# A post-norm transformer layer on 8 cores: the first layernorm's scaling moved out of the row block and into the FFN's accumulation

## What is computed

```python
# layer input x: [16, 2048, 1024]
a = window_attention(x)      # 16 heads of 64, 2 kv heads, window of 256 rows,
                             # softmax without scaling, then @ Wo + bo
x = layernorm(x + a)         # (v - mean) / sqrt(var + 1e-5), no gain, no offset
# FFN: complex linear map, 512 real + 512 imaginary features, no nonlinearity
W_real = unfold(G1_R, G2_R); W_imag = unfold(G1_I, G2_I)        # 512 x 512 each
out_real = x_real @ W_real.T - x_imag @ W_imag.T + bias_real
out_imag = x_real @ W_imag.T + x_imag @ W_real.T + bias_imag
x = layernorm(x + concat(out_real, out_imag))
```

## Time and profile before

| | us |
|---|---|
| median of 3 runs | 1385.72 (1383.74 to 1406.99) |
| the profiled execution | 1384.69, its span on the slowest core (core 2) 1383.1 |
| spans of the eight cores | 1373.1 to 1383.1 |
| mean granted TensorE clock, all cores | 0.75 |
| prologue, until the first scores | 229.7 |

### The profile page before, as it was taken

One profiled execution on the slowest core, in us unless ns is written; L12 is line 12 of the kernel. 1 busy time (PEld: TensorE's weight loads), 2 busy tenths in 40 slices (PEclk: granted clock), 3 DMA queues, 4 the chain that ended last, 5 costly groups with the idle time before them and its releaser, 6 DMA issues.

```text
span 1383.1 us, 17008 instructions; the slowest of 8 cores (1373.1 to 1383.1 us)
## 1 busy us (share of the span) xinstructions
PE 810.7 (59%) x4568; PEld 358.3 (26%) x4568; DVE 557.3 (40%) x1539; ACT 396.1 (29%) x673; POOL 359.3 (26%) x324
## 2 busy tenths in 40 slices
PE   0077333766577666676756476757486557665653
PEld 0033000322233223232222232323232223222321
DVE  0001444355505551455554111455415541555553
ACT  3333113322323322333320234323233223322310
POOL 0000002434304340343430103343214430343410
PEclk9998555677777777877777686777687767777776
DMA  5520000000100001000000300000200020000000
GB/s 135 175 67 31 0 0 1 1 16 31 56 21 17 16 31 61 16 17 16 21 27 16 107 31 1 2 30 17 77 1 17 31 71 7 16 17 31 16 16 31
DMA packets 15869, 44.51 MB, mean 32 GB/s; under 512 B 3091, under 2 KB 5539, under 8 KB 15782
## 3 DMA queue, kind: packets, MB, share of 16 engines
q0 software_dynamic: 9216, 33.56, 6.9%
q1 hardware_dynamic: 6566, 9.87, 2.6%
HBM read 26.65 MB, written 16.78 MB: 31 GB/s over the span
## 4 chain that ended last, share of the span: by engine, by line
PE 52%; DVE 21%; issue 10%; DMA 8%; ACT 5%; POOL 2%; DVEq 1%; SPq 0%; ACTq 0%; POOLq 0%
PE pW L637 11%; PE pW L764 10%; PE pW L411 9%; PE pS L562 5%; DVE scr L650 5%; DMA xs<-x 5%; DVE attn L590 4%; PE pS L505 4%; PE pT L612 2%; PE pT L735 2%; DVE pre L783 2%; DVE x_tm L715 2%; PE pW L768 2%; DVE pre L680 1%; PE pW L641 1%
## 5 line engine op out<-in xcount | busy, mean ns | idle before, releaser
L523 ACT ACTIVATE EX<-pS,expbias 128x512 bf16<-128x512 f32 x384 | 242.6, 682 | 334.0 <-PE pS L505 333.5
L539 POOL TENSOR_TENSOR EX<-EX,maskl_s 128x512 bf16<-128x512 bf16 x128 | 150.7, 1199 | 417.2 <-ACT EX L523 417.2
L539 POOL TENSOR_TENSOR EX<-EX,maskr_s 128x512 bf16<-128x512 bf16 x128 | 172.3, 1369 | 275.0 <-ACT EX L523 274.4
L637 PE MATMUL pW<-wo_sb,attnT 128*128 128x512 bf16 x512 | 174.0, 502 | 34.6 <-DVE pre L783 33.3
L411 PE MATMUL pW<-XT,wq_sb 128*128 128x512 bf16 x512 | 130.6, 423 | 9.0 <-DVE XT L391 9.0
L735 PE MATMUL pT<-identb,x_tm 128*128 128x128 bf16 x256 | 31.2, 298 | 170.7 <-DVE x_tm L715 170.7
L650 DVE SCALAR_TENSOR_TENSOR scr<-pre 128x1024 bf16<-128x1024 f32 x64 | 122.0, 1906 | 6.7
L381 PE MATMUL pT<-identb,x_tm 128*128 128x128 bf16 x256 | 32.0, 304 | 156.0 <-ACT x_tm L371 142.8
L590 DVE TENSOR_SCALAR attn<-pS,Rrec 128x64 bf16<-128x64 f32 x512 | 110.2, 278 | 14.3 <-DVE attn L590 0.5
L505 PE MATMUL pS<-QT,KT 64*128 64x512 bf16 x384 | 102.5, 472 | 13.1 <-ACT EX L523 11.5
L580 DVE RECIPROCAL Rrec<-pS 128x4 f32<-128x4 f32 x128 | 23.3, 182 | 183.6 <-PE pS L562 183.2
(11 more groups left out here) (81 smaller groups left out, 764.3 us busy)
## 6 DMA issues: line engine op xcount, KB each, us to landing
xs<-x POOLq DMA_DIRECT2D x32, 512.0 KB, 4.6
y<-outst POOLq DMA_DIRECT2D x32, 512.0 KB, 3.0
wstage<-wq SPq DMA_DIRECT2D x4, 512.0 KB, 4.0
xs<-wq SPq DMA_DIRECT2D x4, 512.0 KB, 4.5
wstage<-wo SPq DMA_DIRECT2D x4, 512.0 KB, 4.4
xs<-wo SPq DMA_DIRECT2D x4, 512.0 KB, 4.5
wstage<-wk SPq DMA_DIRECT2D x1, 512.0 KB, 4.4
xs<-wv SPq DMA_DIRECT2D x1, 512.0 KB, 4.6
```

Of the source, the lines that this page charges most:

```text
L523: i = sca.activation(EX[:, exi * 512:(exi + 1) * 512], pS[quad % 2][:, :], AF.Exp, bias=expbias[:])
L539: i = gps.tensor_mul(EX[:, exi * 512:(exi + 1) * 512], EX[:, exi * 512:(exi + 1) * 512], m[:]) \
L637: ten.matmul(pW[half][:, :], attnT[:, ring * 1024 + c * 128: ring * 1024 + (c + 1) * 128], wo_sb[:, c * 1024 + half * 512: c * 1024 + (hal ...
```

## The change

The row block is no longer normalised before the FFN. With p the sum x + attention output (kept in bf16 as pre1b), m its mean and r its rstd, the FFN of the normalised rows is r * (p W - m (column sums of W) + beta / r), and a layernorm behind it doesn't see the factor r but in its epsilon. So:

- `x1norm_unit` and x1_tm are gone; the transposes read pre1b, and wait for the add alone. pre1b is bf16 where pre1 was fp32.
- `rstd1_unit` gets three small VectorE operations: -m and 1/r are written side by side as bf16 (spair).
- A new `statT_unit`, ahead of FFN half 0, transposes the two columns on TensorE into one row in pT, and VectorE copies the 256 values to srow.
- Each FFN half gets one more matmul with one contraction row (-m times the column sums of the weights, wbar_row), and the bias is multiplied by 1/r in place of 1.
- The second layernorm's statistics get three small VectorE operations more (the variance times r squared, plus epsilon) and one after rstd2 (r2c = rstd2 * rstd1).
- At the end of `emit_wbuild`, once: 16 matmuls with a column of ones and two ScalarE copies make wbar_row; the first waits for wrt, wit and witn.

```diff
+            for half in range(2):
+                if cur == "t":
+                    E.wait(E.res("pW0b")["f"])
+                    E.wait([ev_wrt, ev_wit, ev_init_v])
+                for c in range(8):
+                    ...
+                    i = ten.matmul(pW[0][0:1, :], ones_col[:],
+                                   wsrc[:, wc * 512:(wc + 1) * 512],
+                                   start=(c == 0), stop=(c == 7)) if cur == "t" else None
+                ev_mm = E.inc("t", i if cur == "t" else None)
+                if cur == "s":
+                    E.wait(ev_mm)
+                    i = sca.copy(wbar_row[0:1, half * 512:(half + 1) * 512], pW[0][0:1, :])
...
         def ln1_unit(b, S):
...
+                    if half == 0:
+                        E.wait(rx1["f"])
                 i = vec.scalar_tensor_tensor(
-                    pre1[:, ring * 1024 + half * 512: ring * 1024 + (half + 1) * 512],
+                    pre1b[:, ring * 1024 + half * 512: ring * 1024 + (half + 1) * 512],
...
+            rx1["r"] = ev_add
...
         def rstd1_unit(b, S):
...
+                vec.tensor_copy(spair[:, ring * 2: ring * 2 + 1], st1[:, c0 + 3:c0 + 4])
+                i = vec.reciprocal(st1[:, c0 + 4:c0 + 5], rstd1[:, ring:ring + 1])
...
+                i = vec.tensor_copy(spair[:, ring * 2 + 1: ring * 2 + 2],
+                                    st1[:, c0 + 4:c0 + 5])
-        def x1norm_unit(b, S):
...
+        def statT_unit(b, S):
+            ring = S % 2
+            rpt = E.res("pT")
+            i = None
+            if cur == "t":
+                E.wait(E.ev[f"spair_{ring}"])
+                E.wait(rpt["f"])
+                ten.transpose(pT[0:1, 0:128], spair[:, ring * 2: ring * 2 + 1],
+                              identb[:])
+                i = ten.transpose(pT[0:1, 128:256], spair[:, ring * 2 + 1: ring * 2 + 2],
+                                  identb[:])
+            ev_tr = E.inc("t", i if cur == "t" else None)
+            i = None
+            if cur == "v":
+                E.wait(ev_tr)
+                i = vec.tensor_copy(srow[0:1, ring * 256: ring * 256 + 256],
+                                    pT[0:1, 0:256])
+            ev_ev = E.inc("v", i)
+            rpt["f"] = ev_ev
+            E.ev[f"srow_{ring}"] = ev_ev
...
         def x1t_unit(b, S):
...
-                                  x1_tm[:, ring * 1024 + c * 128: ring * 1024 + (c + 1) * 128],
+                                  pre1b[:, ring * 1024 + c * 128: ring * 1024 + (c + 1) * 128],
...
         def ffn_unit(b, S, half):
...
+                E.wait(E.ev[f"srow_{ring}"])
...
-            i = ten.matmul(pW[half][:, :], ones_row[:],
+            ten.matmul(pW[half][:, :], srow[0:1, ring * 256: ring * 256 + 128],
+                       wbar_row[0:1, half * 512:(half + 1) * 512],
+                       start=False, stop=False) if cur == "t" else None
+            i = ten.matmul(pW[half][:, :], srow[0:1, ring * 256 + 128: ring * 256 + 256],
                            beta_row[0:1, half * 512:(half + 1) * 512],
                            start=False, stop=True) if cur == "t" else None
...
         def ln2out_unit(b, S):
...
+            extras = [
+                lambda: vec.tensor_tensor(st2[:, c0 + 4:c0 + 5], rstd1[:, ring:ring + 1],
+                                          rstd1[:, ring:ring + 1], ALU.mult),
+                lambda: vec.tensor_tensor(st2[:, c0 + 5:c0 + 6], st2[:, c0 + 6:c0 + 7],
+                                          st2[:, c0 + 4:c0 + 5], ALU.mult),
+                lambda: vec.tensor_scalar(st2[:, c0 + 6:c0 + 7], st2[:, c0 + 5:c0 + 6],
+                                          1.0, EPS, ALU.mult, ALU.add),
+            ]
...
+                i = vec.tensor_tensor(r2c[:, ring:ring + 1], rstd2[:, ring:ring + 1],
+                                      rstd1[:, ring:ring + 1], ALU.mult)
...
                 if 0 <= Q2 < 16:
+                    statT_unit(b, Q2)
                     ffn_unit(b, Q2, 0)
...
                     rstd1_unit(b, P)
-                    x1norm_unit(b, P)
```

83 lines of the change are left out of this document (47 added, 36 removed).

## The result

The changed kernel takes 1473.97 us (median of 10 runs) where the kernel before takes 1385.21 beside it: ratio 1.0643, 95% interval 1.0627 to 1.066. In some executions the cores of one die show a lower granted clock and take a few per cent longer; ratios leave these out. The sign of the forecast holds, its size doesn't: 1430 with a range to 1450. The profiled execution has spans of 1463.3 to 1474.7 us and a mean granted clock of 0.72 where it was 0.75.

A forecast was written before the change was run, and what follows sets the result against it. Waits between engines, then TensorE's clock, were taken to bound the kernel. Covered steps 24, steps after QKV 5.7, batch ends 1 and prologue 14 gave 45 us on 1384.69: 1430 us, +3.2%; range 1396 to 1450 at about 0.85.

The forecast's parts named there:

- the exponentials start at 439.8, as before: One loop step: the square waits only for the first mask and ends at 438.1 (before 438.03), so exponentials are not delayed.
- the 0.4 us that were to be gained before the FFN: One loop step: with normalisation and its wait gone, the FFN starts at 443.5 instead of 443.93.
- the clock's term: Covered steps: the hole ahead of the FFN delays the fast clock by 1.6 to 2.4 us, costing 0.95 us each.
- rival A: The clock rises as before despite the 0.75 us hole ahead of the FFN: 1407 us, +1.5%; chance 0.28.
- If the rise counts from the FFN's start: Clock in one step: counted from the FFN's start at 443.5, the rise comes at 447.0 to 447.8 instead of 445.4.
- Transposes of the statistics to FFN: Ahead of FFN half 0: the two new statistics transposes and their copy cost 0.96 us (0.69 to 1.3).
- The one-row matmuls: One added 512-column matmul in each FFN half: 0.23 us fast each, 0.46 us for a step.
- The prologue: Column sums of the weights ahead of the first scores, paid once: 14.0 us, or 10.6 at the fast clock.
- Steps with a QKV block: Steps after a QKV block, 4 of 32: hole 0.96 plus matmuls 0.46, 1.4 us each, 5.7 in all.
- Batch ends: Four steps at the ends of the two batches: +0.7 for the last, -0.3 for the one before, about 1 us in all.
- B: Rival: the clock doesn't fall at all in TensorE's wait, saving 2.2 us in 24 steps: 1354 us, -2.3%; chance 0.05.
- C: Rival: first layernorm's square runs at twice the rate on 16-bit inputs, 0.53 us less: 1394 or 1417; with A 0.08.

The follow-up runs named there:

- c_delay: Kernel before plus only the change's delay: three one-column VectorE operations behind the second layernorm's variance, one behind its rstd; 1400.5 us, ratio 1.0125.
- b_stat: Kernel before plus only the statistics pair, its two transposes, the copy and the FFN's wait for it, the row unused; 1412.7 us, ratio 1.0217.
- b_k1: Kernel before with each FFN half's bias matmul done twice, one more one-row matmul of 512 columns per half; 1389.7 us, ratio 1.0049.
- c_bare: Changed kernel without column sums, statistics transposes, extra one-row matmuls and the second layernorm's three operations, output differs; 1361.2 us, ratio 0.9843 to the kernel before.
- c_bare_both: Changed kernel without column sums and extra one-row matmuls, keeping the second layernorm's three operations and the statistics transposes; 1421.8 us, ratio 1.0289 to the kernel before.
- a_ysp: Changed kernel with the output DMA issued from SyncE's queue in place of GpSimd's; 1403.7 us, ratio 1.0131 to the kernel before.
- a_noext: Changed kernel without the three small operations in the second layernorm; 1472.3 us, ratio 1.0592 to the kernel before.
- c_bare_ext: Changed kernel without column sums, statistics transposes and extra one-row matmuls, keeping the second layernorm's three operations; 1381.5 us, ratio 0.9993 to the kernel before.
- b_ysp: Kernel before with the output DMA issued from SyncE's queue in place of GpSimd's; 1361.7 us, ratio 0.9841.

## Why the prediction was wrong

**The failed step: "the exponentials start at 439.8, as before."** It let the square end 1.23 us behind the first mask. c_delay shows that it ends 1.10 us behind the second one, and so do the rows of before on which I had built: masks until 434.67 + 2.26 = 436.93, square until 438.03. I had this sum before me and read the 2.39 us as "two masks ran beside it" without asking behind which of them it ended. With it the exponentials are at W + 5.8 and the 0.4 us that were to be gained before the FFN became 0.3 lost. Its own price is 15 us (c_delay), the third part of the miss.

**The larger miss, and the second step that failed, is the clock's term.** I took 0.95 us for each covered step, from a shift of the rise by 1.6 to 2.4 us at half the loss, as if each step were a little longer. The step's net came out at 2.17 and not 1.01, as 119 steps of 30.5 us and 73 of 27.9. The prediction had the warning in one clause ("up to 1.7 if steps fall out of their 27.30 rhythm") and gave it no case of its own. That kind of step is also why rival A (1407) was as wrong: b_stat alone, the hole of rival A's question, has 60 long steps and costs 29 us.

**What caused the hole's price was not what I said.** "If the rise counts from the FFN's start" doesn't hold as a rule: the row at 659.01 of b_stat is fast directly behind the hole, and at 686.00 of the changed kernel the rise came 1.9 us behind the FFN's start and not 3.5 to 4.3. In the short steps it comes after 2.2 us on average, in the long ones after 5.7; so the forecast's 3.5 to 4.3 fits neither kind there, and only b_stat's long steps (4.2) come near it. The rule of the Trainium skill that I had put beside it ("TensorE: Matmul & The Clock Gate", Part 1: The HAM clock gate: the slow state is the default, activity releases it) doesn't contradict either row, but it doesn't give the two kinds of steps, and no number of mine came out of it.

**Terms that were right.** Transposes of the statistics to FFN: 0.96 forecast, 624.85 - 623.94 = 0.91 measured. The wait that takes the place of x_tm's: "TensorE waits for ScalarE's exponentials, some 3.5 us", 4.15 at 621.87. The output block is late and the masks with it: W + 0.72, forecast W + 1.04.

**Terms that were mis-sized.** The one-row matmuls: 0.46 forecast for a step, nothing in b_k1's covered steps (27.24 against 27.32) and 5.7 us in its whole time, though the remainder of 35 us above may say more in the changed kernel's company. The prologue: 14.0 forecast, 10.7 between the slowest cores (first scores at 240.44, 229.74 before), 10.1 as a mean of the eight:

```profile
232.45 1.22 DVE L343 TENSOR_SCALAR witn<-wacc 128x2048 bf16<-128x2048 f32 x1
233.93 1.87 PE L362 MATMUL pW<-wrt,ones_col 128*1 128x512 bf16 x4 [4.45 <-DVE witn L343]
235.59 1.90 PE L362 MATMUL pW<-witn,ones_col 128*1 128x512 bf16 x4
238.62 1.02 PE L362 MATMUL pW<-wit,ones_col 128*1 128x512 bf16 x4 [1.13 <-ACT wbar_row L369]
239.48 1.03 PE L362 MATMUL pW<-wrt,ones_col 128*1 128x512 bf16 x4
240.44 0.39 PE L534 MATMUL pS<-QT,KT 64*128 64x512 bf16 x2
```

The second eight ran at 2.4 GHz, which gives back 1.6 us; I had named the fast clock as the lower bound and taken the slow one. The rest is that the matmuls could start sooner than I had it: witn took 1.22 us where it took 2.17, and the cast to wit ahead of it 1.23 where it took 1.99. In the kernel before, the first step's masks ran beside them:

```profile
231.28 6.55 POOL L539 TENSOR_TENSOR EX<-EX,maskl_s 128x512 bf16<-128x512 bf16 x4 [124.87 <-ACT EX L523]
```

The changed kernel makes its first scores only after the column sums, so no mask runs there yet. Steps with a QKV block: 1.4 forecast, 3.6 measured; I counted only hole and matmuls, though masks and square delay the step behind such a block too (c_delay: 0.95 of it). Batch ends: 1 in all forecast, about 5 measured for the step before the last alone.

**The rivals.** B (the clock never falls) is out: the first scores after the wait take 1.16 us for two at a granted 0.50. C (the square at twice the rate) is out too: the line of the changed kernel has both types, and the least of each is 1225 ns.

```profile
L679 DVE SCALAR_TENSOR_TENSOR scr<-pre1b x32: 1225/3208/3246, 272.3 to 1445.4; 128x1024 bf16<-128x1024 bf16 x32
...
L679 DVE SCALAR_TENSOR_TENSOR scr<-pre x32: 1225/1575/1853, 295.7 to 1460.5; 128x1024 bf16<-128x1024 f32 x32
```

**What stays open.** Shown: the queue behind the output block, the square behind both masks, and that hole and delay make some steps long (on the kernel before each by itself, 60 and 21 of 192; on c_bare 67 with both together, and 8 and 6 just under the limit with one). Not shown: what decides for one step whether it is long. Within a kernel the long steps have the later FFN (W + 9.97 against 9.15 in the changed kernel, 9.84 against 8.95 in c_bare_both, 10.88 against 10.09 in c_delay), but the ranges overlap. It isn't the FFN's start after W alone (a_ysp has 9 long steps at a mean of 8.43, a_noext 117 at 9.02, but c_bare_ext none at 8.39, and the kernel before none at 9.33). And the 35 us of the one-row matmuls in company are a remainder, not a measurement.

## What to carry to other kernels

Before you cost a delay, follow it down the list of the engine that waits: here a few one-column operations held back the output block, the output block a DMA issue, the DMA issue two masks, and the masks the operation on which two other engines wait; the cheapest cure was another queue for the DMA. When a kernel's steps all have one length and a mean clock between the levels, count on prices that are not proportional: here a part cost a step nothing or some three us, and only a version with all parts together told which. An algebraic change that frees TensorE from a wait paid here only once nothing else in the in-order lists still hung on the same statistics: the same change was +6.4% in its first order and -2.5% in its last, of which 1.6 points come with the queue alone (b_ysp) and 0.9 are all that the rest adds.

## What the hardware showed that I had not expected

**VectorE got next to nothing done beside two or four GpSimd operations in a row.** The square alone takes 1225 ns, with two masks 3208, with four 5234 (medians). The Trainium skill ("SBUF — State Buffer", Who interferes with whom) states that a VectorE instruction with two SBUF inputs contends with a GpSimd instruction that reads SBUF, and that the one that issues first has the pair of ports for the whole instruction. The trace agrees, and goes further than that sentence (c_delay, masks from 641.79 to 644.05, square from 641.94 to 645.15): the next mask is taken up before the square that has been waiting since the first.

**Half the bytes, the same time.** The square, with its sum, takes at least 1225 ns on bf16 inputs, as on fp32.

**The same work before it, another clock.** Two steps with the same matmuls in the same order, their FFNs at W + 9.58 and W + 9.40, got the fast clock 8.4 us and 1.9 us behind the FFN's start. The long steps of all kernels average 29.7 to 30.7 us and the short ones 26.1 to 27.9, and a part that delays the FFN by 0.85 us (c_delay) leaves 171 of 192 as long as they were.
